# Weight splits, first loads and one pair's order moved in a five-stage transformer kernel

## What is computed

```python
x = x + tanh(g_xattn[0]) * attention0(layernorm(x), ctx, mask)
    # 16 heads of 32; linear layers with dynamic 8-bit rounding of rows; keys and values from ctx
x = x + tanh(g_ffn[0]) * ffn0(layernorm(x))
    # weights from packed 4-bit numbers with scales per group: h = silu(x Wg) * (x Wu); y = h Wd; y / rms(y)
x = x + tanh(g_xattn[1]) * attention1(layernorm(x), ctx)
    # 16 query heads of 128, 4 key heads; q, k = rms_norm, then rope; keys [ctx, self], causal; out @ wo
x = x + tanh(g_ffn[1]) * moe(layernorm(x))
    # router softmax, best 8 of 64 experts per token, silu(gate) * up, down, weighted sum
```

## The kernel before

| stage | function | us in the trace |
| --- | --- | --- |
| first attention | `layer0_attention` | 0 to 510 |
| FFN | `layer0_ffn` | 510 to 938.2 |
| projections of the second attention | `layer1_projections` | 938.2 to 1383.7 |
| second attention | `layer1_attention` | 1383.7 to about 2410 |

## Time and profile before

### The profile page before, as it was taken

How to read it: one execution, slowest core, us unless ns; L and a number is a source line. 1 busy time by engine, 2 the same in 40 slices (tenths; PEclk the granted TensorE clock), 3 DMA queues, 4 the chain that set the end, 5 groups by cost and what they waited for, 6 DMA issues and landing times. The chain is left out here.

```text
span 2921.2 us, 48636 instructions
## 1 busy us (share of the span) xinstructions
PE 2596.1 (89%) x17264; PEld 2094.4 (72%) x17291; DVE 1705.4 (58%) x3807; ACT 1289.4 (44%) x3413; POOL 874.1 (30%) x877
## 2 busy tenths in 40 slices
PE   7999985699997899998899999999999984598895
PEld 5666753699996688886788888888888873255552
DVE  6767677934343666665666666666666657422221
ACT  4777775222222444443655555555555541121221
POOL 3344322200000455553322222222222220244443
PEclk9999998899998999999899999999999996799997
DMA  3110002400012555556512421421241118799976
GB/s 139 39 48 20 24 26 78 124 30 15 30 37 76 181 187 186 180 189 231 169 44 64 150 78 52 141 66 37 80 124 47 41 33 286 210 295 297 300 191 113
DMA packets 227216, 340.07 MB, mean 116 GB/s; under 512 B 24737, under 2 KB 111137, under 8 KB 226465
## 3 DMA queue, kind: packets, MB, share of 16 engines
q1 hardware_dynamic: 211104, 296.98, 32.2%
q0 software_dynamic: 14912, 39.85, 6.6%
q10 hardware_dynamic: 960, 0.13, 0.0%
HBM read 230.56 MB, written 110.53 MB: 117 GB/s over the span
## 5 line engine op out<-in xcount | busy, mean ns | idle before, releaser
L1973 POOL TENSOR_SCALAR a_prob<-a_prob,a_rinv 128x640 f32<-128x640 f32 (+3 forms) x256 | 253.8, 991 | 765.9 <-DVE a_rinv L2129 765.9
L2119 DVE TENSOR_REDUCE a_mx<-a_s_ps 128x1 f32<-128x640 f32 (+3 forms) x256 | 262.4, 1025 | 270.2 <-PE a_s_ps L2043 263.9
L1997 ACT ACTIVATE a_probT<-a_t_ps 128x512 fp32r<-128x512 f32 (+3 forms) x512 | 237.5, 516 | 363.3 <-PE a_t_ps L2051 363.1
L2135 DVE TENSOR_TENSOR a_probT<-a_t_ps,a_probT 128x512 fp32r<-128x512 f32 (+3 forms) x512 | 276.7, 583 | 46.7 <-ACT a_probT L1997 46.5
L1988 ACT ACTIVATE a_prob<-a_s_ps,a_nb,a_rs 128x640 f32<-128x640 f32 (+3 forms) x256 | 268.2, 1048 | 0.0
L137 PE MATMUL a_o_ps<-a_probT,a_v 128*128 128x256 f32 x832 | 245.2, 295 | 0.0
L138 PE MATMUL a_o_ps<-a_probT,a_v 128*128 128x256 f32 x832 | 233.2, 280 | 0.0
L139 PE MATMUL a_o_ps<-a_probT,a_v 128*128 128x256 f32 x832 | 233.0, 280 | 0.0
L2051 PE MATMUL a_t_ps<-h_ident,a_prob 128*128 128x128 f32 x1664 | 225.2, 274 | 4.4 <-POOL a_prob L1973 2.1
L2051 PEld LDWEIGHTS a_t_ps<-h_ident,a_prob 128*128 128x128 f32 x1664 | 194.5, 141 | 27.0 <-POOL a_prob L1973 2.8
L715 PE MATMUL a_bank<-a_ident,a_prob 128*128 128x128 f32 x1024 | 161.9, 287 | 38.8 <-ACT a_prob L570 29.5
(11 more groups left out here) (321 smaller groups left out, 7107.2 us busy)
## 6 DMA issues: line engine op xcount, KB each, us to landing
m_ring<-in_w_gate SPq DMA_DIRECT2D x64, 384.0 KB
m_ring<-in_w_up SPq DMA_DIRECT2D x64, 384.0 KB
m_ring<-in_w_down SPq DMA_DIRECT2D x64, 384.0 KB
l_q_hi<-p_turned SPq DMA_DIRECT2D x64, 256.0 KB, 2.4
...
```

Of the source, the lines that this page charges most:

```text
L1973: pool.tensor_scalar(prob[:, k % 4, 0:w], prob[:, k % 4, 0:w], rinv[:, k % 4:k % 4 + 1], 1.0, ALU.mult, ALU.mult).then_inc(s["weighted"], 1)
L1997: act.activation(probT[0][:, pair % 2, i * 4:i * 4 + n, k % 2], t_ps[i][:, 0:n * P].rearrange("p (m n) -> p m n", n=P), ACT.Copy).then_inc ...
L2119: step(dve.tensor_reduce(mx[:, k % 4:k % 4 + 1], s_ps[:, k % 2, 0:w], AX.X, ALU.max))
L2135: dve.tensor_tensor(probT[1][:, pair % 2, i * 4:i * 4 + n, k % 2], t_ps[i][:, 0:n * P].rearrange("p (m n) -> p m n", n=P), probT[0][:, pai ...
```

## The change

First attention: words and scales of pieces 0 and 1, and words 2, are loaded one tile earlier; scales 2 and 3 at the last two tiles; the last x is stored after all weight transfers. The three operations of `make_whole` become functions of their own, and those of pieces 0 to 2 stand one by one in groups 55 to 63, between two copies. ACT splits the highs of pieces 0 to 2 in groups 64 and 65, the rest after the loop; DVE makes pieces 3, 4, 5 in a row; POOL does the low of piece 3.

FFN, last unit: highs at blocks 2, 5, 8, lows at 3, 6, 9, and the layer norm of the projections' first tile at block 4, with its root on POOL.

Projections: the tables for queries come first in SP's order, those for keys later; POOL multiplies them in two steps; weights of chunks 3 and 4 are split ahead of the loop, the others five chunks ahead; the ten loads of `next_loads` are issued by ACT at chunks 4, 5 and 6 of the last tile.

Second attention: the gate's tanh moves to k = 16; at k mod 16 = 4 PE weighs before it projects.

The core of the diff:

```diff
@@ -392 +392 @@
-                    if t == TILES - 3:
+                    if t == TILES - 4:
@@ -404,7 +404,3 @@
-                for n in (2, 3):
-                    ffn["load_scale"](sp, n)
-                    if n == 2:
-                        ffn["load_words"](sp, 3)
-                    else:
-                        ffn["load_words"](sp, 4)
-                store(TILES - 1)
+                    if t >= TILES - 2:
+                        ffn["load_scale"](sp, t - (TILES - 2) + 2)
+                ffn["load_words"](sp, 3)
@@ -411,0 +408 @@
+                ffn["load_words"](sp, 4)
@@ -413,0 +411 @@
+                store(TILES - 1)
@@ -522,0 +521 @@
+                ffn["split_low"](pool, 3)
@@ -613,2 +612,7 @@
-                    if G > GROUPS0:
-                        ffn["split_high"](act, G - GROUPS0 - 1)
+                    if G == GROUPS0:
+                        act.wait_ge(s["job_done"], number[last_value(B - 1)])
+                        act.wait_ge(s["job_done"], number[last_key(B - 1)])
+                        ffn["split_high"](act, 0)
+                        ffn["split_high"](act, 1)
+                    if G == GROUPS0 + 1:
+                        ffn["split_high"](act, 2)
@@ -624 +628,2 @@
-                ffn["split_high"](act, DRAIN0 - 1)
+                for n in range(3, EARLY0):
+                    ffn["split_high"](act, n)
@@ -912,0 +918,10 @@
+                    if G == GROUPS0 - 10:
+                        ffn["left_shift"](dve, step)
+                    if GROUPS0 - 9 <= G < GROUPS0:
+                        n = (G - (GROUPS0 - 9)) // 3
+                        if G % 3 == (GROUPS0 - 9) % 3:
+                            ffn["shift_bits"](dve, step, n)
+                        elif G % 3 == (GROUPS0 - 8) % 3:
+                            ffn["mask_bits"](dve, step, n)
+                        else:
+                            ffn["scale_bits"](dve, n)
@@ -932,5 +946,0 @@
-                    if G == GROUPS0:
-                        dve.wait_ge(s["job_done"], number[last_value(B - 1)])
-                        dve.wait_ge(s["job_done"], number[last_key(B - 1)])
-                        ffn["left_shift"](dve, step)
-                        ffn["make_whole"](dve, step, 0)
@@ -938,3 +948 @@
-                        for n in range(EARLY0):
-                            if n + 1 < EARLY0:
-                                ffn["make_whole"](dve, step, n + 1)
+                        for n in range(3):
@@ -941,0 +950,6 @@
+                        ffn["make_whole"](dve, step, 3)
+                        ffn["make_whole"](dve, step, 4)
+                        ffn["make_whole"](dve, step, 5)
+                        dve.wait_ge(h["s"]["split_lo"], 4)
+                        ffn["split_low"](dve, 4)
+                        ffn["split_low"](dve, 5)
...
@@ -1043,2 +1056,7 @@
-        step(dve.tensor_scalar(part, part, h["left"][:], 6, ALU.logical_shift_left, ALU.arith_shift_right))
-        step(dve.tensor_scalar(part, part, FP4_BITS, None, ALU.bitwise_and))
+        step(dve.tensor_scalar(bits(n), bits(n), h["left"][:], 6, ALU.logical_shift_left, ALU.arith_shift_right))
+
+    def mask_bits(dve, step, n):
+        step(dve.tensor_scalar(bits(n), bits(n), FP4_BITS, None, ALU.bitwise_and))
+
+    def scale_bits(dve, n):
+        part = bits(n)
...
@@ -1165,0 +1189,2 @@
+                    else:
+                        root(m["ve"], m["rstd"], var_ready, rstd_ready, UNITS * SUB)
@@ -1223,2 +1248,2 @@
-                        if u == UNITS - 1 and i in (6, 8, 10):
-                            nxt["high"](act, (i - 6) // 2)
+                        if u == UNITS - 1 and i in (2, 5, 8):
+                            nxt["high"](act, i // 3)
@@ -1352,2 +1377,4 @@
-                        if u == UNITS - 1 and i in (7, 9):
-                            nxt["low"](dve, (i - 7) // 2)
+                        if u == UNITS - 1 and i in (3, 6, 9):
+                            nxt["low"](dve, i // 3 - 1)
+                        if u == UNITS - 1 and i == 4:
+                            layer_norm(dve, step, var_ready, rstd_ready, UNITS * SUB, early["x"][:, 0], m, nxt["first_normed"])
@@ -1359 +1385,0 @@
-                nxt["low"](dve, 2)
...
@@ -1565,6 +1592,8 @@
-                def next_loads():
-                    for g in range(1, G1):
-                        load_keys(sp, early, scr, 0, g)
-                        if g < 3:
-                            load_queries(sp, early, scr, g)
-
+                half = HD // 2
+                sp.dma_start(cosw[:, 0], d["cos"].rearrange("(t p) n -> p t n", p=P)).then_inc(s["q_tables_loaded"], 16)
+                sp.dma_start(nw[:, 0], row_of(d["L1_q_norm"], 0, HD)).then_inc(s["q_tables_loaded"], 16)
+                sp.dma_start(sinw[:, 0], d["sin"].rearrange("(t p) n -> p t n", p=P)).then_inc(s["q_tables_loaded"], 16)
+                sp.dma_start(nwr[:, 0, 0:half], row_of(d["L1_q_norm"], half, half)).then_inc(s["q_tables_loaded"], 16)
+                sp.dma_start(nwr[:, 0, half:], row_of(d["L1_q_norm"], 0, half)).then_inc(s["q_tables_loaded"], 16)
+                weights["load"](sp, 2 * SHARED_CH + 2)
+                weights["load"](sp, 2 * SHARED_CH + 3)
@@ -1572,7 +1601,3 @@
-                for i, n in enumerate(("L1_q_norm", "L1_k_norm")):
-                    half = HD // 2
-                    sp.dma_start(nw[:, i], row_of(d[n], 0, HD)).then_inc(s["tables_loaded"], 16)
-                    sp.dma_start(nwr[:, i, 0:half], row_of(d[n], half, half)).then_inc(s["tables_loaded"], 16)
-                    sp.dma_start(nwr[:, i, half:], row_of(d[n], 0, half)).then_inc(s["tables_loaded"], 16)
-                sp.dma_start(cosw[:, 0], d["cos"].rearrange("(t p) n -> p t n", p=P)).then_inc(s["tables_loaded"], 16)
-                sp.dma_start(sinw[:, 0], d["sin"].rearrange("(t p) n -> p t n", p=P)).then_inc(s["tables_loaded"], 16)
+                sp.dma_start(nw[:, 1], row_of(d["L1_k_norm"], 0, HD)).then_inc(s["k_tables_loaded"], 16)
+                sp.dma_start(nwr[:, 1, 0:half], row_of(d["L1_k_norm"], half, half)).then_inc(s["k_tables_loaded"], 16)
+                sp.dma_start(nwr[:, 1, half:], row_of(d["L1_k_norm"], 0, half)).then_inc(s["k_tables_loaded"], 16)
...
@@ -1597 +1621,0 @@
-                next_loads()
@@ -1642,5 +1666 @@
-                rstd(0)
-                pool.wait_ge(s["tables_loaded"], 8 * 16)
-                for table, by in ((cosw, nw), (sinw, nwr)):
-                    pool.tensor_tensor(table[:, 1], table[:, 0], by[:, 1:2].to_broadcast([P, NT, HD]), ALU.mult).then_inc(s["tables_k"], 1)
-                pool.wait_ge(s["tables_k"], 2)
+                pool.wait_ge(s["q_tables_loaded"], 5 * 16)
@@ -1648 +1668 @@
-                    pool.tensor_tensor(table[:, 0], table[:, 0], by[:, 0:1].to_broadcast([P, NT, HD]), ALU.mult).then_inc(s["tables_q"], 1)
+                    pool.tensor_tensor(table[:, 1], table[:, 0], by[:, 0:1].to_broadcast([P, NT, HD]), ALU.mult).then_inc(s["tables_q"], 1)
@@ -1652,0 +1673,5 @@
+                    if g == 0:
+                        pool.wait_ge(s["tables_q"], 2)
+                        pool.wait_ge(s["k_tables_loaded"], 3 * 16)
+                        for table, by in ((cosw, nw), (sinw, nwr)):
+                            pool.tensor_tensor(table[:, 0], table[:, 0], by[:, 1:2].to_broadcast([P, NT, HD]), ALU.mult).then_inc(s["tables_k"], 1)
@@ -1678,0 +1704,12 @@
+                def next_loads(ch):
+                    if ch == SHARED_CH + 1:
+                        for slot in range(RING_T):
+                            act.wait_ge(t_stored[slot], 32 * (NT * TURNED // RING_T))
+                        load_keys(act, early, scr, 0, 1)
+                    elif ch == SHARED_CH + 2:
+                        load_queries(act, early, scr, 1)
+                        load_keys(act, early, scr, 0, 2)
+                    elif ch == SHARED_CH + 3:
+                        load_queries(act, early, scr, 2)
+                        load_keys(act, early, scr, 0, 3)
+
@@ -1679,0 +1717,2 @@
+                weights["high"](act, SHARED_CH)
+                weights["high"](act, SHARED_CH + 1)
@@ -1705,2 +1744,2 @@
-                        if ck + SHARED_CH < CHUNKS:
-                            weights["high"](act, ck + SHARED_CH)
+                        if ck + SHARED_CH + 2 < CHUNKS:
+                            weights["high"](act, ck + SHARED_CH + 2)
@@ -1708,0 +1748,2 @@
+                    if g == TILES - 1:
+                        next_loads(ch)
...
@@ -1835,2 +1876,3 @@
-                statistics(0)
-                norm(0)
+                dve.sem_inc(s["var_ready"], 1)
+                dve.sem_inc(s["rstd_ready"], 1)
+                dve.sem_inc(s["normed"], 1)
...
@@ -1841,0 +1886,2 @@
+                        if ck == Q_CHUNKS:
+                            dve.wait_ge(s["tables_k"], 2)
...
@@ -2010,2 +2055,0 @@
-                act.wait_ge(s["gate_loaded"], 16)
```

(13 more changed lines are left out.)

29 lines of the change are left out of this document (18 added, 11 removed).

## The result

The changed kernel takes 2895.41 us (median of four runs, 2892.45 to 2898.07) against 2927.45 for the kernel before (four runs too). The ratio estimated from the runs is 0.9894, with a 95% interval of 0.9871 to 0.9916; the two medians give 0.9891. That is 32.0 us faster, as forecast; the forecast time of 2893 is missed by 2.4 us, by which the median before, with a fourth run, had risen as well. The profiled execution took 2892.45 with a span of 2890.7, 30.5 us shorter than before. The sum is right, but not each of its terms, and this table says where they went.

What follows compares the result with a forecast made beforehand. TensorE was busy for 89% of the span, so the question was which of its waits go. 4.1 + 8.8 + 6.5 + 1.5 + 11.1 = 32.0 us off 2922.97 gives 2891.0; plus 2.06 for the median, 2893, range 2879 to 2907.

Steps and rivals of the forecast that it cites:

- A: End of the first attention, up to the FFN: last DVE split at 505.5 instead of 509.6, gain 4.1 us (bounds 2.5 to 7.5).
- The step on the moved operations: First attention, groups 55 to 63: nine operations moved into DVE's idle time cost nothing; 5.9 us if that cover were gone.
- Rival 4: First attention: the moved operations lengthen each group, gain 4.1 − 5.9, time 2899 us; chance 0.08.
- the chain: End of the first attention: words 3 near 491.5, then pieces 3, 4, 5 made in turn, two splits, end at 505.5.
- The 1.3 us for POOL's work beside piece 3: End of the first attention: estimated addition to the 2.67 us of making piece 3, between nothing and 2.06.
- B: FFN's last unit: earlier highs and lows remove the 9.3 us lost in down projections, gain 8.8 us (bounds 5 to 9.4).
- The half microsecond of waiting that I put back: FFN's last unit: 0.5 us of PE waiting for lows of blocks 8 to 10, subtracted from the 9.3 us.
- C: Projections' first tile: second tile starts 43.6 us after the stage's start instead of 50.1, gain 6.5 us (bounds 2.2 to 10).
- D: Between projections and second attention: loads moved to ACT's queue, gate's tanh later; gain 1.5 us (ends −4 and +8).
- a bound by volume: Before the second attention: 15.7 MB at 0.32 MB/us from 1361 us puts wo piece 3 at 1410, gain at most 3.
- Rival 1: Between projections and second attention: shared transfers hold back the last stores, −6.5 instead of 1.5 us, time 2901; chance 0.15.
- E: Inside the second attention: 15 waits for DVE's add, 0.76 us each, go; gain 11.1 us (10 to 11.4).

Runs made afterwards that it cites:

- order_only: The kernel before with only the second attention's new order (at k mod 16 = 4 weighing ahead of projection): 2913.67 us, 0.9959 of the kernel before.
- loads_back: The changed kernel with the ten loads of keys and queries back on SP behind its loop, the late gate tanh kept: 2895.08 us.
- changed_again: The changed kernel unaltered, run once more beside two other kernels on the same chip: 2895.63 us, 0.9905 of the kernel before (seven runs).
- gate_back: The changed kernel with the gate's tanh back ahead of the first exp, the loads still on ACT's queue: 2899.34 us (one run).

## Why the prediction was right, and where it was not

**A, 4.1 forecast, 3.9 measured.** The step on the moved operations held: the last product of the first attention came 1.7 us later, but that offset of about 2 us stands in DVE's timeline already at 305 us, a hundred microseconds before the first moved operation, and groups 55 to 63 add nothing to it. Rival 4 is out. Less 1.7, the last split ended at 505.7, against 505.5 forecast, with the mask beside POOL at 2.71 as against 2.75. But inside the chain two errors cancel. The 1.3 us for POOL's work beside piece 3 didn't come (its operations took 0.75, 0.69 and 1.22), so piece 3 was whole 1.9 us before its mark. Then DVE waited 1.52 us for the words of piece 4, which the chain lacked, and its shift took 1.55 instead of 0.75. (By the terms as written piece 4 ends at 500.2, not 500.4.)

**B, 8.8 forecast, 10.0.** The mechanism is right. The half microsecond of waiting that I put back didn't come. The down projections also began 0.6 us earlier in the unit, but so they did in `order_only` without part B: it is the pace of the matmuls in this unit (last section), 0.118 us in the kernel before, 0.113 in the changed one. At equal pace part B is worth 9.6 (55.3 against 45.7) or 9.1 (55.7 against 46.6 in `loads_back`). So 0.4 to 0.9 of the 10.0 is luck.

**C, 6.5 forecast, 7.4.** The second tile started 42.5 us after the stage, not 43.6, and PE's last wait before it was for the key item, as said (0.75 us). The constants came as forecast, 2.2 us (7.1 instead of 9.3). In the middle I let PE go on from chunk to chunk; in fact it stood once, for 8.9 us, for the second tile's norm, which stands in DVE's row behind the lows. And I read the tables wrongly: I let DVE's first rope go near 946, 7.8 us after the stage's start, and it went after 12.9 (14.6 before), since DVE's row has the lows of chunks 3 and 4 ahead of it. The lead carries the part: without it, norm and tables together gained nothing.

**D, 1.5 forecast, −3.8 in that profile.** The step that failed is "9.7 MB ... is 30.3 us, 1391 instead of 1383.7 ... I take 1.5": the stage did start later, 6.4 us against 7.3 forecast, the first exp followed 3.7 us later, as forecast, and `wo` 3 is what both kernels waited for, as written. But the gain was then read from a bound by volume, as if the transfers would come in the best order. With the loads on ACT's queue the high of `wo` 3 comes about 1.2 us later, not 1.5 earlier. In the profile of the table it is 1.1, and the other 2.7 us of the −3.8 stand between this high and the first add, 55.3 against 52.6 us, at a granted clock of 0.94 against 1.00. In `changed_again`, at 1.00, the whole stretch took 99.3 us, as before (99.7). Rival 1 described the mechanism, with too high a price. The rule of the Trainium skill ("DMA: Bandwidth & Descriptors", Issuing engines are not separate DMA queues), that such a move saves only the time to issue, fits: moving the loads back cost nothing (`loads_back`, 2895.08). In this kernel they also pushed back stores on which a stage's end hung, whose longest landing went from 5.8 to 11.6 us.

**E, 11.1 forecast, 14.2,** above the end of 11.4 that I gave. The step that was mis-sized is the term "15 waits, 11.4 us, 0.76 each": 0.76 is idle time in the record; the waits cost 0.95 from start to start.

**The rest.** 3.5 us in the FFN before unit 7 and −1.7 and −3.2 elsewhere belong to no edit. They nearly cancel: −1.5 in all. The 3.5 goes with the pace of the matmuls: this stretch took 364.0 to 365.1 us in the three profiles without slow units after the first, and 366.4 to 369.1 in the eleven in which every other unit is slow, the kernel before among them. Part of what made the sum right to 1 us is thus luck: D fell short by 5.3, and B, C and E brought 5.2 more than said.

**Still open:** what makes the granted clock fall between the high of `wo` 3 and the first add in some executions and not in others with the same code; what sets the pace of the FFN's units; and why the second key scaling came after 67.1 us in `gate_back` and 64.5 in the changed kernel, whose code is the same there.
